# Pairwise products of 40 projected features: two input buffers and growing stores, against four input buffers and twelve equal stores a tile

## The chip, the cores and the metric

The kernel runs on one core of a Trainium2 chip, the others idle. The metric is the device time in microseconds (us) of one execution. Before the change the median of three runs is 506.32 us (506.20 to 506.38). The profiled execution took 506.18 us, of which the profile's span covers 504.4 us.

## The reference

The input `r_x` is 512 x 40 x 128 in float32 and `W` is 128 x 128. Each of the 40 features of a sample is projected with `W`, and the output holds the elementwise product of each of the 780 pairs of projected features:

```
proj = jnp.einsum('bnd,ed->bne', x, W)          # 512 x 40 x 128
out = proj[:, PAIR_I, :] * proj[:, PAIR_J, :]   # 512 x 780 x 128, pairs i < j
```

The input has 10.5 MB, the output 204.5 MB.

## The kernel before

The 512 samples are cut into four tiles of 128, one sample to a partition. The five engines run programs written out by hand, and semaphores alone set the order between them.

**Loads.** SyncE (SP in the profile) issues all transfers but that of W. Tile 0 is loaded in three pieces (`FIRST_LOADS`), then tile 1 (L111). `feats` has two halves; tile t lives in half t % 2. Tiles 2 and 3 are loaded later (L122): SP issues each once all stores of tile t - 2 are issued, since the products of that tile were then computed and its half is free. They stand in the same queue as the stores.

**Projection.** TensorE turns two features at a time (L140), ScalarE carries them to SBUF (L189), TensorE multiplies them by the turned W (L149), and ScalarE writes the result over the features in `feats` (L195). This goes in groups of two features from feature 39 down. From tile 1 on, TensorE waits for the tile's load first (L173).

**Products.** VectorE (DVE) goes through the pairs from the last to the first. Pairs with one i are one instruction (L212), cut where a chunk ends. A chunk is what one store moves. It is written into one of three slots (`products0` to `products2`), and VectorE waits before each chunk until the store that last used its slot has landed (L222 in tile 0, L227 in the loop over tiles 1 to 3). For tile 0 there are 15 chunks that grow from 30 to 69 pairs (`FIRST_SIZES`), for each later tile nine chunks of 87 or 86 pairs (`SIZES`).

**Stores.** SP waits until a chunk is ready (L117) and issues its store (L118), 42 stores in all. One pair of one tile is 64 KB (128 partitions x 512 bytes). SP waits for the last three stores at the end (L126).

Of the kernel before, what the change touches and what calls it, by code (L numbers as in the profile page):

```python
# [5 lines left out]
P = 128  # L6
FEATURES = 40
DIM = 128
PAIRS = FEATURES * (FEATURES - 1) // 2
FIRST_PAIR = [i * (FEATURES - 1) - i * (i - 1) // 2 for i in range(FEATURES)]  # L10

GROUP = 2
# [4 lines left out]
FIRST_LOADS = [(36, 40), (28, 36), (0, 28)]  # L17

SLOTS = 3
FIRST_SIZES = [30, 34, 38, 41, 44, 47, 50, 53, 56, 59, 62, 64, 66, 67, 69]
SIZES = [87] * 6 + [86] * 3
SLOT_PAIRS = max(FIRST_SIZES + SIZES)
FIRST_ROUNDS = len(FIRST_SIZES) // SLOTS
ROUNDS = len(SIZES) // SLOTS

assert sum(FIRST_SIZES) == PAIRS and sum(SIZES) == PAIRS
assert FIRST_ROUNDS * SLOTS == len(FIRST_SIZES) and ROUNDS * SLOTS == len(SIZES)
assert GROUPS * GROUP == FEATURES and GROUPS % 2 == 0 and GROUP <= BANK_FEATURES  # L30


# [5 lines left out]
    return (FEATURES - 1 - i) // GROUP  # L38


def chunk_ranges(sizes):

    ranges, high = [], PAIRS
    for size in sizes:
        ranges.append((high - size, high))
        high -= size
    return ranges


def chunk_rows(low, high):  # L50

    rows = []
    for i in reversed(range(FEATURES - 1)):
        a, b = max(low, FIRST_PAIR[i]), min(high, FIRST_PAIR[i + 1])
        if a < b:
            rows.append((i, i + 1 + a - FIRST_PAIR[i], b - a, a - low))
    return rows


def pairwise_products(nc, x, w, out):  # L60
    fp32 = mybir.dt.float32
    ALU = mybir.AluOpType
    tiles = x.shape[0] // P
    assert x.shape[0] == tiles * P and tiles % 2 == 0 and tiles >= 4

    first_chunks = chunk_ranges(FIRST_SIZES)
    chunks = chunk_ranges(SIZES)

    with ExitStack() as ctx:  # L69
        def sbuf(name, shape):  # L70
            return ctx.enter_context(nc.sbuf_tensor(name, shape, fp32))
# [4 lines left out]
        def sem(name):  # L76
            return ctx.enter_context(nc.semaphore(name))


        feats = sbuf("feats", [P, 2, FEATURES, DIM])  # L80
        products = [sbuf(f"products{s}", [P, SLOT_PAIRS, DIM]) for s in range(SLOTS)]
        x_turned = [sbuf(f"x_turned{k}", [DIM, GROUP, P]) for k in range(2)]
        w_in = sbuf("w_in", [DIM, DIM])
        w_turned = sbuf("w_turned", [DIM, DIM])
        identity = sbuf("identity", [P, P])
# [4 lines left out]

        w_loaded = sem("w_loaded")
        first_loaded = [sem(f"first_loaded{k}") for k in range(len(FIRST_LOADS))]
        tile_loaded = [sem(f"tile_loaded{half}") for half in range(2)]
        identity_zeroed = sem("identity_zeroed")
        identity_made = sem("identity_made")
        w_in_ps = sem("w_in_ps")
# [10 lines left out]
        @block.sync  # L107
        def _(sp):
            for k, (a, b) in enumerate(FIRST_LOADS):
                sp.dma_start(feats[:, 0, a:b, :], x[0:P, a:b, :]).then_inc(first_loaded[k], 16)  # L110
            sp.dma_start(feats[:, 1, :, :], x[P:2 * P, :, :]).then_inc(tile_loaded[1], 16)  # L111

            done = 0
            for tile in range(tiles):
                for k, (a, b) in enumerate(first_chunks if tile == 0 else chunks):
                    done += 1
                    sp.wait_ge(chunk_ready, done)  # L117
                    sp.dma_start(out[tile * P:(tile + 1) * P, a:b, :],  # L118
                                 products[k % SLOTS][:, 0:b - a, :]).then_inc(stored[k % SLOTS], 16)
                if tile + 2 < tiles:  # L120

                    sp.dma_start(feats[:, tile % 2, :, :],  # L122
                                 x[(tile + 2) * P:(tile + 3) * P, :, :]).then_inc(tile_loaded[tile % 2], 16)

            for slot in range(SLOTS):
                sp.wait_ge(stored[slot], 16 * (FIRST_ROUNDS + (tiles - 1) * ROUNDS))  # L126

        @block.gpsimd
        def _(pool):
# [4 lines left out]

        @block.tensor
        def _(pe):
            def turn(half, group):
                a, b = group_range(group)
                for n in range(a, b):
                    last = pe.transpose(turned_ps[group % 2][:, n - a, :], feats[:, half, n, :], identity[:, :])  # L140
                last.then_inc(group_turned, 1)

            def project(before, group):
                pe.wait_ge(x_turned_ready, before + (group + 1))
                if group >= 2:

                    pe.wait_ge(proj_ready, before + (group - 1))
                for k in range(GROUP):
                    last = pe.matmul(proj_ps[group % 2][:, k, :], x_turned[group % 2][:, k, :], w_turned[:, :],  # L149
                                     start=True, stop=True)  # L150
                last.then_inc(group_projected, 1)

            def last_banks_left(before):
                pe.wait_ge(proj_ready, before + GROUPS)

            pe.wait_ge(identity_made, 1)
            pe.wait_ge(w_loaded, 16)
            pe.transpose(w_ps[:, :], w_in[:, :], identity[:, :]).then_inc(w_in_ps, 1)  # L158

            starts = {group_of(b - 1): k for k, (a, b) in enumerate(FIRST_LOADS)}  # L160
            pe.wait_ge(first_loaded[0], 16)
            turn(0, 0)
            pe.wait_ge(w_ready, 1)
            for group in range(1, GROUPS):
                if group in starts:
                    pe.wait_ge(first_loaded[starts[group]], 16)
                turn(0, group)
                project(0, group - 1)
            project(0, GROUPS - 1)
            last_banks_left(0)  # L170

            for tile in range(1, tiles):
                pe.wait_ge(tile_loaded[tile % 2], 16 * ((tile + 1) // 2) if tile % 2 else 16 * (tile // 2))  # L173
                turn(tile % 2, 0)
                for group in range(1, GROUPS):
                    turn(tile % 2, group)
                    project(tile * GROUPS, group - 1)
                project(tile * GROUPS, GROUPS - 1)
                last_banks_left(tile * GROUPS)

        @block.scalar
        def _(act):
            act.dma_start(w_in[:, :], w).then_inc(w_loaded, 16)
            act.wait_ge(w_in_ps, 1)
            act.copy(w_turned[:, :], w_ps[:, :]).then_inc(w_ready, 1)  # L185

            def carry_turned(tile, group):
                act.wait_ge(group_turned, tile * GROUPS + group + 1)
                act.copy(x_turned[group % 2][:, :, :], turned_ps[group % 2][:, 0:GROUP, :]).then_inc(x_turned_ready, 1)  # L189

            def carry_projected(tile, group):

                a, b = group_range(group)
                act.wait_ge(group_projected, tile * GROUPS + group + 1)
                act.copy(feats[:, tile % 2, a:b, :], proj_ps[group % 2][:, 0:GROUP, :]).then_inc(proj_ready, 1)  # L195

            for tile in range(tiles):
                carry_turned(tile, 0)
                for group in range(1, GROUPS):
                    carry_turned(tile, group)  # L200
                    carry_projected(tile, group - 1)
                carry_projected(tile, GROUPS - 1)

        @block.vector
        def _(dve):
            def multiply_chunk(tile, k, low, high, seen):

                for i, j, count, place in chunk_rows(low, high):
                    if group_of(i) >= seen:
                        seen = group_of(i) + 1  # L210
                        dve.wait_ge(proj_ready, tile * GROUPS + seen)  # L211
                    last = dve.tensor_tensor(  # L212
                        products[k % SLOTS][:, place:place + count, :],
                        feats[:, tile % 2, i:i + 1, :].broadcast_to([P, count, DIM]),
                        feats[:, tile % 2, j:j + count, :], ALU.mult)
                last.then_inc(chunk_ready, 1)
                return seen

            seen = 0
            for k, (low, high) in enumerate(first_chunks):  # L220
                if k >= SLOTS:
                    dve.wait_ge(stored[k % SLOTS], 16 * (k // SLOTS))  # L222
                seen = multiply_chunk(0, k, low, high, seen)
            with dve.Fori(1, tiles) as tile:  # L224
                seen = 0
                for k, (low, high) in enumerate(chunks):
                    dve.wait_ge(stored[k % SLOTS],  # L227
                                16 * ROUNDS * tile + 16 * (FIRST_ROUNDS - ROUNDS + k // SLOTS))
                    seen = multiply_chunk(tile, k, low, high, seen)


# [19 lines left out]
```

## Time and profile before

| what | value |
|---|---|
| median of 3 runs | 506.32 us |
| profiled execution, its own time | 506.18 us |
| span of its profile | 504.4 us |
| VectorE busy | 431.6 us (86%) |
| TensorE busy / ScalarE busy | 66.4 us / 54.7 us |
| moved by the DMA engines | 215.11 MB, 426 GB/s over the span |
| read from HBM / written to HBM | 10.55 MB / 204.47 MB |
| VectorE waiting for a store to land | 36.6 us |
| SP waiting for a chunk of products | 457.7 us |

A queue's share in the profile is the time that its packets took, divided by the time that 16 DMA engines have in the span: close to 100% means that the engines hardly ever stood still. SP's wait for products is no loss by itself, since SP waits while earlier stores are still being moved. The GB/s of a short stretch is rough by a few GB/s, because a store's packets are large (43.5 KB in a store of 87 pairs) and 16 of them are under way at a time.

### The profile page before, as it was taken

How to read it: one execution, taken by the hardware profiler on the slowest of the kernel's cores; microseconds unless marked ns; L12 is line 12 of the kernel's file. 1: busy time of each engine (PE TensorE's matmuls, PEld its weight loads, DVE VectorE, ACT ScalarE, POOL GpSimd, SP SyncE). 2: the span in 40 equal slices, each digit the busy share in tenths (PEclk: the TensorE clock that was granted, in tenths of full speed). 3: DMA queues.
4: the chain of work that ended last, by engine and by line, in shares of the span. 5: the costliest groups of instructions: out<-in, count | busy, mean ns of one | idle time of the engine just before them, and what ended most of it. 6: DMA issues, size and time to landing. Idle time of an engine off the chain costs nothing.

```text
span 504.4 us, 1671 instructions
## 1 busy us (share of the span) xinstructions
PE 66.4 (13%) x481; PEld 60.9 (12%) x481; DVE 431.6 (86%) x191; ACT 54.7 (11%) x162; POOL 0.7 (0%) x6
## 2 busy tenths in 40 slices
PE   6990000000067000000007500000000000000000
PEld 6880000000057000000007500000000000000000
DVE  3999999999996989888996788988899998988800
ACT  5880000000036000000005500000000000000000
POOL 0000000000000000000000000000000000000000
PEclk9995555555559555555557955555555555555555
DMA  8999999999999999999999999999999999999997
GB/s 350 428 435 425 429 434 432 444 428 437 384 404 439 442 424 435 442 435 419 440 421 455 413 439 445 420 435 441 433 423 440 442 424 435 442 427 429 440 443 307
DMA packets 7062, 215.11 MB, mean 426 GB/s; under 512 B 784, under 2 KB 912, under 8 KB 1168
## 3 DMA queue, kind: packets, MB, share of 16 engines
q1 hardware_dynamic: 6912, 214.96, 99.3%
q10 hardware_dynamic: 144, 0.07, 0.0%
q8 instruction: 4, 0.07, 0.0%
q14 instruction: 2, 0.02, 0.0%
HBM read 10.55 MB, written 204.47 MB: 426 GB/s over the span
## 4 chain that ended last, share of the span: by engine, by line
DMA 46%; DVE 41%; issue 5%; DVEq 2%; PE 1%; ACT 0%
DMA out_dram<-products 45%; DVE products L212 41%; DVEq L69 1%; DMA w_in<-in_L_rec_W_dram 1%; PE proj_ps L149 1%; DVEq L212 0%; PE turned_ps L140 0%; DVEq L211 0%; DVEq L224 0%; PE w_ps L158 0%; ACT feats L195 0%; DVEq L227 0%
## 5 line engine op out<-in xcount | busy, mean ns | idle before, releaser
L212 DVE TENSOR_TENSOR products<-feats 128x384 f32 (+49 forms) x191 | 431.6, 2331 | 45.1 <-DMA out_dram<-products 36.6
L140 PE MATMUL turned_ps<-identity,feats 128*128 128x128 f32 x160 | 33.3, 297 | 213.8 <-DMA feats<-in_r_x_dram 213.3
L149 PE MATMUL proj_ps<-w_turned,x_turned 128*128 128x128 f32 x320 | 56.9, 304 | 0.3 <-ACT x_turned L189 0.2
L189 ACT COPY x_turned<-turned_ps 128x256 f32<-128x256 f32 x80 | 30.1, 378 | 215.3 <-PE turned_ps L140 214.8
L140 PEld LDWEIGHTS turned_ps<-identity,feats 128*128 128x128 f32 x160 | 22.1, 156 | 214.6 <-issue 213.6
L149 PEld LDWEIGHTS proj_ps<-w_turned,x_turned 128*128 128x128 f32 x320 | 45.5, 205 | 4.8 <-ACT x_turned L189 2.0
L195 ACT COPY feats<-proj_ps 128x256 f32<-128x256 f32 x80 | 29.8, 372 | 11.8 <-PE proj_ps L149 6.6
L185 ACT ACT_TABLE_LOAD x1 | 1.3, 1283 | 1.2 <-PEq L240 1.2
L158 PE MATMUL w_ps<-identity,w_in 128*128 128x128 f32 x1 | 0.4, 444 | 4.1 <-DMA w_in<-in_L_rec_W_dram 4.1
L158 PEld LDWEIGHTS w_ps<-identity,w_in 128*128 128x128 f32 x1 | 0.2, 183 | 4.1 <-issue 4.1
L185 ACT COPY w_turned<-w_ps 128x128 f32<-128x128 f32 x1 | 0.3, 265 | 2.2 <-PE w_ps L158 2.2
L132 POOL TENSOR_SCALAR_AFFINE_SELECT identity<-identity 128x128 f32<-128x128 f32 x1 | 0.3, 293 | 0.2 <-POOL identity L130 0.2
L130 POOL MEMSET identity<- 128x128 f32 x1 | 0.2, 205 | 0.3 <-POOLq L240 0.3
L240 POOL MEMSET const-bfloat16-1.0<- 128x1 bf16 x1 | 0.1, 101 | 0.0
L240 POOL MEMSET const-uint8-127<- 128x1 uint8 x1 | 0.1, 101 | 0.0
L240 POOL MEMSET const-float32-0.0<- 128x1 f32 x1 | 0.1, 98 | 0.2 <-issue 0.2
L240 POOL MEMSET const-float32-1.0<- 128x1 f32 x1 | 0.1, 98 | 0.0
## 6 DMA issues: line engine op xcount, KB each, us to landing
out_dram<-products SPq DMA_DIRECT2D x18, 5568.0 KB, 27.5
out_dram<-products SPq DMA_DIRECT2D x9, 5504.0 KB, 27.3
feats<-in_r_x_dram SPq DMA_DIRECT2D x3, 2560.0 KB, 26.8
out_dram<-products SPq DMA_DIRECT2D x1, 4416.0 KB, 18.9
out_dram<-products SPq DMA_DIRECT2D x1, 4288.0 KB, 17.7
out_dram<-products SPq DMA_DIRECT2D x1, 4224.0 KB, 16.7
out_dram<-products SPq DMA_DIRECT2D x1, 4096.0 KB, 15.8
out_dram<-products SPq DMA_DIRECT2D x1, 3968.0 KB, 14.8
```

The source lines that it names most:

```text
L69: with ExitStack() as ctx:
L130: pool.memset(identity[:, :], 0.0).then_inc(identity_zeroed, 1)
L132: pool.affine_select(out=identity[:, :], in_=identity[:, :], compare_op=ALU.not_equal, fill=1.0, base=0, pattern=[[-1, P]], channel_multip ...
L140: last = pe.transpose(turned_ps[group % 2][:, n - a, :], feats[:, half, n, :], identity[:, :])
L149: last = pe.matmul(proj_ps[group % 2][:, k, :], x_turned[group % 2][:, k, :], w_turned[:, :], start=True, stop=True)
L158: pe.transpose(w_ps[:, :], w_in[:, :], identity[:, :]).then_inc(w_in_ps, 1)
L185: act.copy(w_turned[:, :], w_ps[:, :]).then_inc(w_ready, 1)
L189: act.copy(x_turned[group % 2][:, :, :], turned_ps[group % 2][:, 0:GROUP, :]).then_inc(x_turned_ready, 1)
L195: act.copy(feats[:, tile % 2, a:b, :], proj_ps[group % 2][:, 0:GROUP, :]).then_inc(proj_ready, 1)
L212: last = dve.tensor_tensor(products[k % SLOTS][:, place:place + count, :], feats[:, tile % 2, i:i + 1, :].broadcast_to([P, count, DIM]), f ...
L240: nc = _bacc.Bacc("TRN2", target_bir_lowering=False, num_devices=1)
```

## The change

`feats` gets one buffer per tile, four in all. SP issues the loads of tiles 1, 2 and 3 directly behind those of tile 0, all on one semaphore, `tiles_loaded`, and no load between the stores. TensorE waits once, before tile 1, until all three have landed. A tile's projections are written over its own buffer, as before. All tiles have the same twelve chunks of 65 pairs, so there are 48 stores; the three slots shrink from 87 to 65 pairs. Pairs, products and their order are the same.

```diff
-FIRST_SIZES = [30, 34, 38, 41, 44, 47, 50, 53, 56, 59, 62, 64, 66, 67, 69]
-SIZES = [87] * 6 + [86] * 3
+CHUNK = 65
+CHUNKS = PAIRS // CHUNK
+ROUNDS = CHUNKS // SLOTS
...
-        feats = sbuf("feats", [P, 2, FEATURES, DIM])
-        products = [sbuf(f"products{s}", [P, SLOT_PAIRS, DIM]) for s in range(SLOTS)]
+        feats = sbuf("feats", [P, tiles, FEATURES, DIM])
+        products = [sbuf(f"products{s}", [P, CHUNK, DIM]) for s in range(SLOTS)]
...
-            sp.dma_start(feats[:, 1, :, :], x[P:2 * P, :, :]).then_inc(tile_loaded[1], 16)
-            done = 0
+            for tile in range(1, tiles):
+                sp.dma_start(feats[:, tile, :, :], x[tile * P:(tile + 1) * P, :, :]).then_inc(tiles_loaded, 16)
...
-                if tile + 2 < tiles:
-                    sp.dma_start(feats[:, tile % 2, :, :],
-                                 x[(tile + 2) * P:(tile + 3) * P, :, :]).then_inc(tile_loaded[tile % 2], 16)
...
+            pe.wait_ge(tiles_loaded, 16 * (tiles - 1))
             for tile in range(1, tiles):
-                pe.wait_ge(tile_loaded[tile % 2], 16 * ((tile + 1) // 2) if tile % 2 else 16 * (tile // 2))
...
-                for k, (low, high) in enumerate(chunks):
-                    dve.wait_ge(stored[k % SLOTS],
-                                16 * ROUNDS * tile + 16 * (FIRST_ROUNDS - ROUNDS + k // SLOTS))
-                    seen = multiply_chunk(tile, k, low, high, seen)
+                for k in range(CHUNKS):
+                    dve.wait_ge(stored[k % SLOTS], 16 * ROUNDS * tile + 16 * (k // SLOTS))
+                    seen = multiply_chunk(tile, k, seen)
```

The queue of SP before, from the load of tile 1 into the stores of tile 1; 128x3840 is a store of 30 pairs (128 elements each):

```order
L111 DMA feats<-in_r_x_dram 128x5120
L118 DMA out_dram<-products 128x3840 [waits chunk_ready]
L118 DMA out_dram<-products 128x4352 [waits chunk_ready]
...
L118 DMA out_dram<-products 128x8576 [waits chunk_ready]
L118 DMA out_dram<-products 128x8832 [waits chunk_ready]
L122 DMA feats<-in_r_x_dram 128x5120
L118 DMA out_dram<-products 128x11136 [waits chunk_ready] x6
```

The whole queue of SP in the changed kernel:

```order
L96 UNCONDITIONAL_BRANCH [waits barrier_Pool_Activation_PE_DVE_SP_release]
L99 DMA feats<-in_r_x_dram 128x512
L99 DMA feats<-in_r_x_dram 128x1024
L99 DMA feats<-in_r_x_dram 128x3584
L101 DMA feats<-in_r_x_dram 128x5120 x3
L107 DMA out_dram<-products 128x8320 [waits chunk_ready] x48
L57 UNCONDITIONAL_BRANCH [waits stored2,stored1,stored0]
```

The two later loads moved ahead of the first store, and the stores became 48 equal ones.

VectorE's first chunk before ends with the row of 128x256 (1 + 2 + ... + 7 + 2 = 30 pairs):

```order
L212 TENSOR_TENSOR products<-feats 128x640
L212 TENSOR_TENSOR products<-feats 128x768 [waits proj_ready]
L212 TENSOR_TENSOR products<-feats 128x896
L212 TENSOR_TENSOR products<-feats 128x256 [waits proj_ready]
L212 TENSOR_TENSOR products<-feats 128x768
L212 TENSOR_TENSOR products<-feats 128x1152
```

In the changed kernel it ends with the first of the two rows of 128x1280 (1 + 2 + ... + 10 + 10 = 65 pairs):

```order
L197 TENSOR_TENSOR products<-feats 128x640
L197 TENSOR_TENSOR products<-feats 128x768 [waits proj_ready]
L197 TENSOR_TENSOR products<-feats 128x896
L197 TENSOR_TENSOR products<-feats 128x1024 [waits proj_ready]
L197 TENSOR_TENSOR products<-feats 128x1152
L197 TENSOR_TENSOR products<-feats 128x1280 [waits proj_ready]
L197 TENSOR_TENSOR products<-feats 128x1280
```

The products are computed in the same order, and the point at which the first store may go moved from the 30th pair to the 65th.

## Rows read from the trace of the kernel before

**Rows 1.** The page's DMA rows: the span in 40 slices, then queue q1.
```profile
DMA  8999999999999999999999999999999999999997
GB/s 350 428 435 425 429 434 432 444 428 437 384 404 439 442 424 435 442 435 419 440 421 455 413 439 445 420 435 441 433 423 440 442 424 435 442 427 429 440 443 307
...
q1 hardware_dynamic: 6912, 214.96, 99.3%
```

**Rows 2.** SP's timeline, single windows: start us, us, the DMA issued.
```profile
13.25 0.35 SPq L118 DMA_DIRECT2D out_dram<-products  x1
...
18.05 0.34 SPq L118 DMA_DIRECT2D out_dram<-products  x1
...
116.72 1.24 SPq L122 DMA_DIRECT2D feats<-in_r_x_dram  x1
...
476.76 0.33 SPq L118 DMA_DIRECT2D out_dram<-products  x1
```

**Rows 3.** Waits of VectorE and SP in total: us, times, longest us.
```profile
DVE products L212 <- DMA out_dram<-products: 36.6, 22, 7.5
...
SPq L126 <- DMA out_dram<-products: 26.8, 1, 26.8
```

**Rows 4.** Stretches: length, each engine's busy us, PEclk, DMA share, GB/s.
```profile
2.00:27.00 25.00, 22.17 (x161) 20.14 (x161) 18.60 (x19) 17.86 (x54) 0.00 (x0) 1.00 1.02 425
...
27.00:130.00 103.00, 10.18 (x83) 9.22 (x81) 103.00 (x50) 9.21 (x29) 0.00 (x0) 0.56 1.01 432
...
115.00:145.00 30.00, 1.32 (x5) 0.95 (x6) 30.00 (x23) 0.61 (x2) 0.00 (x0) 0.50 1.02 411
...
130.00:145.00 15.00, 1.32 (x5) 0.95 (x6) 15.00 (x8) 0.61 (x2) 0.00 (x0) 0.50 1.01 384
...
245.00:280.00 35.00, 12.09 (x85) 11.37 (x86) 27.64 (x15) 9.08 (x28) 0.00 (x0) 0.62 0.99 425
...
270.00:480.00 210.00, 14.64 (x114) 13.75 (x112) 182.62 (x69) 12.58 (x38) 0.00 (x0) 0.54 1.00 434
```

**Rows 5.** The page's DMA issues: count, KB each, median us from issue to landing.
```profile
out_dram<-products SPq DMA_DIRECT2D x18, 5568.0 KB, 27.5
...
feats<-in_r_x_dram SPq DMA_DIRECT2D x3, 2560.0 KB, 26.8
...
out_dram<-products SPq DMA_DIRECT2D x1, 4224.0 KB, 16.7
```

**Rows 6.** VectorE's timeline: start us, us, instructions, idle before and its releaser.
```profile
183.18 11.89 DVE L212 TENSOR_TENSOR products<-feats 128x3840 f32 x3 [1.40 <-DMA out_dram<-products]
196.12 11.83 DVE L212 TENSOR_TENSOR products<-feats 128x768 f32 x4 [1.04 <-DMA out_dram<-products]
209.25 11.76 DVE L212 TENSOR_TENSOR products<-feats 128x2816 f32 x3 [1.30 <-DMA out_dram<-products]
222.39 11.76 DVE L212 TENSOR_TENSOR products<-feats 128x1152 f32 x3 [1.38 <-DMA out_dram<-products]
235.79 24.82 DVE L212 TENSOR_TENSOR products<-feats 128x128 f32 x20 [1.63 <-DMA out_dram<-products]
261.38 12.03 DVE L212 TENSOR_TENSOR products<-feats 128x2048 f32 x5 [0.77 <-DMA out_dram<-products]
```

**Rows 7.** VectorE's instructions by shape: busy us in total, mean ns of one.
```profile
L212 DVE TENSOR_TENSOR products<-feats 128x4992 f32 x3 | 16.1, 5351 | 0.0
...
L212 DVE TENSOR_TENSOR products<-feats 128x1920 f32 x6 | 12.9, 2155 | 12.5 <-DMA out_dram<-products 12.5
```

**Rows 8.** Timeline of TensorE and ScalarE: tile 1's first turn, tile 3's last copy.
```profile
21.86 0.66 PE L140 MATMUL turned_ps<-identity,feats 128*128 128x128 f32 x4 [0.46 <-ACT feats L195]
...
284.70 0.37 ACT L195 COPY feats<-proj_ps 128x256 f32<-128x256 f32 x1 [0.36 <-PE proj_ps L149]
```

More of the change, by code:

```diff
@@ L21 @@
 SLOTS = 3
-FIRST_SIZES = [30, 34, 38, 41, 44, 47, 50, 53, 56, 59, 62, 64, 66, 67, 69]
-SIZES = [87] * 6 + [86] * 3
[L24 to L29, printed above, removed]
+CHUNK = 65
+CHUNKS = PAIRS // CHUNK
+ROUNDS = CHUNKS // SLOTS
+assert CHUNKS * CHUNK == PAIRS and ROUNDS * SLOTS == CHUNKS
 assert GROUPS * GROUP == FEATURES and GROUPS % 2 == 0 and GROUP <= BANK_FEATURES
@@ L38, in group_of, with chunk_range @@
     return (FEATURES - 1 - i) // GROUP
[L41 to L47, printed above, removed]
+def chunk_range(k):
+    return PAIRS - (k + 1) * CHUNK, PAIRS - k * CHUNK
 def chunk_rows(low, high):
@@ L63, in pairwise_products @@
     tiles = x.shape[0] // P
-    assert x.shape[0] == tiles * P and tiles % 2 == 0 and tiles >= 4
-    first_chunks = chunk_ranges(FIRST_SIZES)
-    chunks = chunk_ranges(SIZES)
+    assert x.shape[0] == tiles * P and 2 <= tiles <= 4
     with ExitStack() as ctx:
@@ L92, in pairwise_products @@
         first_loaded = [sem(f"first_loaded{k}") for k in range(len(FIRST_LOADS))]
-        tile_loaded = [sem(f"tile_loaded{half}") for half in range(2)]
+        tiles_loaded = sem("tiles_loaded")
         identity_zeroed = sem("identity_zeroed")
@@ L110, in _ @@
                 sp.dma_start(feats[:, 0, a:b, :], x[0:P, a:b, :]).then_inc(first_loaded[k], 16)
-            sp.dma_start(feats[:, 1, :, :], x[P:2 * P, :, :]).then_inc(tile_loaded[1], 16)
-            done = 0
+            for tile in range(1, tiles):
+                sp.dma_start(feats[:, tile, :, :], x[tile * P:(tile + 1) * P, :, :]).then_inc(tiles_loaded, 16)
             for tile in range(tiles):
[L115 to L119, printed above, removed]
-                if tile + 2 < tiles:
-                    sp.dma_start(feats[:, tile % 2, :, :],
-                                 x[(tile + 2) * P:(tile + 3) * P, :, :]).then_inc(tile_loaded[tile % 2], 16)
+                for k in range(CHUNKS):
+                    low, high = chunk_range(k)
+                    sp.wait_ge(chunk_ready, tile * CHUNKS + k + 1)
+                    sp.dma_start(out[tile * P:(tile + 1) * P, low:high, :],
+                                 products[k % SLOTS][:, :, :]).then_inc(stored[k % SLOTS], 16)
             for slot in range(SLOTS):
-                sp.wait_ge(stored[slot], 16 * (FIRST_ROUNDS + (tiles - 1) * ROUNDS))
+                sp.wait_ge(stored[slot], 16 * tiles * ROUNDS)
         @block.gpsimd
@@ L136, in _, with turn @@
         def _(pe):
-            def turn(half, group):
+            def turn(tile, group):
                 a, b = group_range(group)
                 for n in range(a, b):
-                    last = pe.transpose(turned_ps[group % 2][:, n - a, :], feats[:, half, n, :], identity[:, :])
+                    last = pe.transpose(turned_ps[group % 2][:, n - a, :], feats[:, tile, n, :], identity[:, :])
                 last.then_inc(group_turned, 1)
@@ L170, in _ @@
             last_banks_left(0)
+            pe.wait_ge(tiles_loaded, 16 * (tiles - 1))
             for tile in range(1, tiles):
-                pe.wait_ge(tile_loaded[tile % 2], 16 * ((tile + 1) // 2) if tile % 2 else 16 * (tile // 2))
-                turn(tile % 2, 0)
+                turn(tile, 0)
                 for group in range(1, GROUPS):
-                    turn(tile % 2, group)
+                    turn(tile, group)
                     project(tile * GROUPS, group - 1)
@@ L194, in carry_projected @@
                 act.wait_ge(group_projected, tile * GROUPS + group + 1)
-                act.copy(feats[:, tile % 2, a:b, :], proj_ps[group % 2][:, 0:GROUP, :]).then_inc(proj_ready, 1)
+                act.copy(feats[:, tile, a:b, :], proj_ps[group % 2][:, 0:GROUP, :]).then_inc(proj_ready, 1)
             for tile in range(tiles):
@@ L205, in _, with multiply_chunk @@
         def _(dve):
-            def multiply_chunk(tile, k, low, high, seen):
-                for i, j, count, place in chunk_rows(low, high):
+            def multiply_chunk(tile, k, seen):
+                for i, j, count, place in chunk_rows(*chunk_range(k)):
                     if group_of(i) >= seen:
@@ L213, in multiply_chunk @@
                         products[k % SLOTS][:, place:place + count, :],
-                        feats[:, tile % 2, i:i + 1, :].broadcast_to([P, count, DIM]),
-                        feats[:, tile % 2, j:j + count, :], ALU.mult)
+                        feats[:, tile, i:i + 1, :].broadcast_to([P, count, DIM]),
+                        feats[:, tile, j:j + count, :], ALU.mult)
                 last.then_inc(chunk_ready, 1)
@@ L219, in _ @@
             seen = 0
-            for k, (low, high) in enumerate(first_chunks):
+            for k in range(CHUNKS):
                 if k >= SLOTS:
                     dve.wait_ge(stored[k % SLOTS], 16 * (k // SLOTS))
-                seen = multiply_chunk(0, k, low, high, seen)
+                seen = multiply_chunk(0, k, seen)
             with dve.Fori(1, tiles) as tile:
                 seen = 0
-                for k, (low, high) in enumerate(chunks):
-                    dve.wait_ge(stored[k % SLOTS],
-                                16 * ROUNDS * tile + 16 * (FIRST_ROUNDS - ROUNDS + k // SLOTS))
-                    seen = multiply_chunk(tile, k, low, high, seen)
+                for k in range(CHUNKS):
+                    dve.wait_ge(stored[k % SLOTS], 16 * ROUNDS * tile + 16 * (k // SLOTS))
+                    seen = multiply_chunk(tile, k, seen)
 _INS = ["r_x", "L0_rec_W"]
```

## The prediction

> **What bounds the kernel now.** I read the page's DMA rows first. Queue q1, which carries all loads of x and all stores, holds the 16 DMA engines for 99.3% of the span, and every slice but the first and the last reads 9 [rows 1]. Then I asked who waits. VectorE waits 36.6 us in all for stores to land [rows 3], so it is not the bound; SP issues the last store at 476.76 us and then waits 26.8 us for it [rows 2, 3]. So the bound is the stream of bytes through the DMA engines, from the first load to the last store. The reader should see that both kernels move the same 10.5 MB in and 204.5 MB out. The change can act on the time only in three ways: the stream runs dry, its rate changes, or its start and end change.
>
> The third view is the rate by stretch [rows 4]. The stream runs at 434 GB/s from 270 to 480 us, where stores of 86 and 87 pairs go, and at 432 from 27 to 130 us, where tile 0's smaller stores go. It dips twice, at the two places where a load passes between stores. From 130 to 145 us it is 384, the low slices 384 and 404 of the page [rows 1]. As the stretch ahead of it reads high (packets are counted whole), I use both together: 411 from 115 to 145 us. SP issued tile 2's load at 116.72 us [rows 2], and loads land 26.8 us after their issue in the middle one of three [rows 5], so about 143 us. The dip ends when the load does. Tile 3's load leaves a much smaller mark: 425 from 245 to 280 us.
>
> **The change part by part.** All sums are made against the span of 504.4 us. The profiled execution took 506.18 us, so 1.8 us lie around its span, and it is 0.14 us under the median of 506.32.
>
> *The loads of tiles 2 and 3 leave the stores.* Their 5.2 MB move to the start, where only loads are under way; their own time moves along and is no gain. The gain is the dips. Tile 2's: 30 us at 411 instead of 434 GB/s is 30 x 23 / 434 = 1.6 us, against 432 it is 1.5 us. Tile 3's: 35 x 9 / 434 = 0.7 us at most; by the row's roughness (one round of 16 packets of 43.5 KB is 0.7 MB, so 20 GB/s over 35 us) it may as well be nothing, and 0.1 is what I take for it. That the dip belongs to mixing load and stores, and not to the reading of tile 2 as such, is not shown by the trace: tile 3's load, in the same position, hardly dips. If it belongs to the tile, it comes again at the start. The bounds are 0 and 2.3 us of gain. I take 1.6.
>
> *Six more stores.* There were 42, there are 48, all of 65 pairs (4.26 MB). Does a smaller store move more slowly per byte? The lower bound is nothing: the 434 GB/s of the large ones holds. The upper bound is the 432 of tile 0's stores, which average 52 pairs (and of which the one nearest in size, 66 pairs, shows nothing special: 16.7 us from issue to landing, with part of its predecessor ahead of it [rows 5]). Tiles 1 to 3 write 153.4 MB: 153.4 / 432 - 153.4 / 434 = 355.0 - 353.4 = 1.6 us. A part of the 432 may stem from something else in that stretch, so I take the middle, 0.8 us of loss.
>
> *A rule against this change.* Between stores of 87 pairs VectorE's waits end every 13.1 us (starts 183.18, 196.12, 209.25, 222.39) [rows 6], and 5.70 MB in 13.1 us is 434 GB/s, so nothing is paid between one store and the next that is queued behind it. The Trainium skill, DMA: Bandwidth & Descriptors, section "Anatomy of one DMA", gives each DMA about 2.0 us fixed beside bytes / 436 GB/s; if these added up in the queue, six more stores would cost 12 us as an estimate from that page. The trace says that this fixed part lies beside the next store: it is seen in landings only, 27.5 us for two times 13.1, thus 1.2 us.
>
> *Does the stream run dry at the start?* Before, the first store is issued at 13.25 us, when the 5.2 MB of two tiles are through [rows 2]. Now 10.5 MB are ahead: at the 425 GB/s of the first stretch [rows 4] they last 24.7 us from 2 us on, to about 27 us. The first chunk ends at pair 65; before, the 64th pair's store went out at 18.05 us [rows 2], and the order of products is the same, so the first store is issued at about 18.2 us, 9 us early. The second needs one more chunk. An instruction costs 1.04 ns per element and 0.16 us (5351 ns for 4992 elements, 2155 for 1920) [rows 7], so a chunk of 8320 elements is 8.7 us and 3 to 11 instructions: 9.1 to 10.4 us. It is ready at 27.5, while the first store lasts until 27 + 9.8 = 37 us.
>
> *Does it run dry later?* A store of 65 pairs takes 4.26 / 434 = 9.8 us. A slot is free when its store has landed, 1.2 us after its last byte; two stores, of 19.6 us, are then queued, so VectorE has 19.6 - 1.2 = 18.4 us for the next chunk. It needs 9.1 to 10.4. Before it had 26.3 - 1.2 = 25.1 and needed 11.8 to 12.4 (24.82 us for the two chunks at a tile's start, with 20 instructions) [rows 6]. The margin falls from 13 to 8 us and covers what lies around a chunk: the idle rows ahead of a chunk are 0.8 to 1.6 us [rows 6]. Cost: nothing. VectorE's waits shrink by nothing that matters either.
>
> *TensorE's single wait.* It started tile 1 at 21.86 us [rows 8]; now it waits until all loads have landed, at 28 to 29 us. Behind that wait stand all turns and products of tiles 1 to 3, and ScalarE's copies. VectorE needs the first of tile 1 only after 780 pairs, thus after its twelfth chunk, about 115 us or later. A tile takes TensorE 16 us (tile 1: about 22 to 38), so all are done near 80 us, instead of 284.70 [rows 8]. Cost: nothing, hidden behind tile 0's products.
>
> *The end.* SP issues the last store about 21 us before the end instead of 26.8; the queue is full until then and the landing of 1.2 us is the same. No gain.
>
> *Sum.* 504.4 - 1.6 + 0.8 = 503.6 us of span, 505.4 as the profiled execution counts, and 505.5 beside the median of 506.32. That is 0.16% less, and a measurement of this kernel can't tell less than 0.2% (1.0 us) from no change. The forecast is: no change that can be measured, with the gain of the unmixed loads half eaten by smaller stores.
>
> **The rivals.** *Faster, 504.7 us.* Small stores go at 434 as well, and both dips go: 506.32 - 1.6 = 504.7, and 504.0 if tile 3's whole 0.7 counts. For it: a fixed price between stores is nowhere seen, and queued loads alone show no dip. Against it: the 432 of tile 0.
>
> *Slower, 507.9 us.* The dip is tile 2's read and comes again, and stores of 65 pairs go at tile 0's rate throughout: 506.32 + 1.6. It decides from 507.3 on, thus when the dip stays and small stores cost at least 1.0 us. For it: tile 3's load in the same place shows nearly no dip, so mixing alone does not explain tile 2's. Against it: the three runs agree within 0.2 us, and the dip lasts just as long as a load.
>
> *Slower by a dry stream, 509 to 515 us.* If VectorE needs more than the 18.4 us for a chunk, each us beyond is lost on every such chunk. At each start of the loop over tiles (three times) a loss of 1 to 3 us would give 3 to 9 us. It needs 8 us above the 10.4 of the longest chunk; no row shows idle time of this size except 7.5 us once, waiting for a store [rows 3].
>
> *The dip stays and small stores are free*: 506.3, no change, like the forecast in the time.
>
> **How the numbers follow.** Dip gone, 0.65; stores of 65 pairs dearer by over 0.8 us, 0.45. This gives: faster (dip gone, stores free or nearly) 0.36; dip gone and stores dear, 505.5 to 506.3, 0.28; dip stays, stores free, 0.18; both against it, 0.14; dry stream 0.04. The second and third lie within 0.2%, with 0.02 of the first: forecast of no change 0.45, faster than 505.3 us 0.38, slower than 507.3 us 0.17. The range leaves out the dry stream and the ends of the others: 504.4 to 507.9 us.
>
> **What would show it.** In the changed profile q1's share stays at 99%, the slice digits are all 9, the landing of a store is 19.6 + 1.2 = 20.8 us, and the first three slices hold all loads. No slice in the middle falls under 410 GB/s if mixing was the cause; a low slice within the first 27 us would show that tile 2's read itself is slow. The rate in the middle is 434 if small stores are free and 432 if not. The forecast is wrong by a dry stream if SP's waits end and DMA digits under 9 stand in the middle, above all at a tile's start.

## The result and the profile after

The changed kernel takes 505.76 us (median of 22 runs, 505.34 to 506.02), the kernel before 506.46 in as many runs beside it (505.94 to 506.99). The ratio is 0.9987, its 95% interval 0.9981 to 0.9993: faster by 0.7 us, or 0.13%. That is clear of zero, though it is less than the 0.2% that the prediction took for the smallest change that can be told. The profiled execution has a span of 503.8 us (504.4 before).

The page's DMA rows of the changed kernel, in 40 slices of 12.6 us, and queue q1:

```profile
DMA  8999999999999999999999999999999999999997
GB/s 356 424 403 441 427 424 429 447 428 425 434 444 428 428 433 444 428 428 431 447 428 428 431 447 428 428 431 441 433 428 428 436 439 431 428 428 439 433 433 312
...
q1 hardware_dynamic: 7776, 214.96, 99.3%
```

As in [rows 1], the stream of bytes is the bound, and all slices but the outer two read 9. The low slices 384 and 404 are gone from the middle. A low slice, 403, now stands at 25 to 38 us.

The rate by stretch of the changed kernel; the columns are those of [rows 4]:

```profile
15.00:21.00 6.00, 5.96 (x48) 5.35 (x46) 6.00 (x5) 5.05 (x16) 0.00 (x0) 1.00 1.02 437
21.00:27.00 6.00, 0.00 (x0) 0.00 (x0) 6.00 (x5) 0.37 (x1) 0.00 (x0) 0.79 1.05 385
...
24.00:30.00 6.00, 0.00 (x0) 0.00 (x0) 6.00 (x5) 0.00 (x0) 0.00 (x0) 0.54 0.99 355
...
115.00:145.00 30.00, 0.00 (x0) 0.00 (x0) 27.84 (x20) 0.00 (x0) 0.00 (x0) 0.50 1.02 438
...
245.00:280.00 35.00, 0.00 (x0) 0.00 (x0) 32.29 (x25) 0.00 (x0) 0.00 (x0) 0.50 1.00 433
270.00:480.00 210.00, 0.00 (x0) 0.00 (x0) 192.60 (x80) 0.00 (x0) 0.00 (x0) 0.50 1.00 433
```

Against [rows 4]: 115 to 145 us went from 411 to 438, 245 to 280 from 425 to 433. The long stretch of stores went from 434 to 433. The new dip is at 21 to 30 us, in the last of the three large loads; the one before it, at 15 to 21 us, runs at 437. The size of a dip can be read from such a row only roughly: a second profile of the changed kernel (g3 below) has 409 where this one has 385. From here on the text therefore also uses the packet records of the traces, the start, size and duration of each packet. A packet of these loads has 20480 bytes and takes 761 ns in the median. "Slow" is one that takes over 60 ns more than is usual for its size, and the sum of such excess, divided by the 16 engines, is what a stall cost.

Landings, waits and VectorE's rhythm after the change, from the page's DMA issues, the waits in total and VectorE's timeline:

```profile
out_dram<-products SPq DMA_DIRECT2D x48, 4160.0 KB, 20.5
```
```profile
DVE products L197 <- DMA out_dram<-products: 41.1, 42, 5.4
...
PE turned_ps L125 <- DMA feats<-in_r_x_dram: 10.3, 1, 10.3
...
SPq L111 <- DMA out_dram<-products: 20.2, 1, 20.2
```
```profile
119.70 8.89 DVE L197 TENSOR_TENSOR products<-feats 128x3328 f32<-128x3328 f32 x2 [0.89 <-DMA out_dram<-products]
129.87 18.65 DVE L197 TENSOR_TENSOR products<-feats 128x128 f32 x17 [1.27 <-DMA out_dram<-products]
149.18 9.10 DVE L197 TENSOR_TENSOR products<-feats 128x768 f32 x5 [0.66 <-DMA out_dram<-products]
159.02 9.03 DVE L197 TENSOR_TENSOR products<-feats 128x1920 f32 x4 [0.74 <-DMA out_dram<-products]
```

VectorE starts a chunk every 9.84 us, as long as a store lasts, and waits 0.7 to 1.3 us before it [rows 6 before: 0.8 to 1.6]. Where 17 instructions stand together, at a tile's start, two chunks take 18.65 us. TensorE's one wait of 10.3 us is seen and nobody waits for it: VectorE's two waits for projections, 8.0 us in all, are both in tile 0, before 9 us.

### The profile page after: what moved, and what is told of

It reads as the page before. It is cut to its first block, busy times and chain, and to the rows that moved or that the text cites. A ratio compares the mean times of both kernels' runs of the same rounds, so it can differ in the third digit from the quotient of the medians.

```text
span 503.8 us, 1684 instructions
## 1 busy us (share of the span) xinstructions
PE 63.4 (13%) x481; PEld 57.6 (11%) x481; DVE 433.6 (86%) x196; ACT 54.2 (11%) x162; POOL 0.7 (0%) x6
## 3 DMA queue, kind: packets, MB, share of 16 engines
q1 hardware_dynamic: 7776, 214.96, 99.3%
## 4 chain that ended last, share of the span: by engine, by line
DMA 62%; DVE 25%; issue 5%; DVEq 2%; PE 1%; ACT 0%
DMA out_dram<-products 62%; DVE products L197 25%; DVEq L57 2%; DMA w_in<-in_L_rec_W_dram 1%; PE proj_ps L134 0%; PE turned_ps L125 0%; DVEq L197 0%; DVEq L196 0%; DVEq L209 0%; PE w_ps L143 0%; ACT feats L180 0%; DVEq L212 0%
## 5 line engine op out<-in xcount | busy, mean ns | idle before, releaser
L197 DVE TENSOR_TENSOR products<-feats 128x1280 f32 (+36 forms) x196 | 433.6, 2275 | 49.2 <-DMA out_dram<-products 41.1
L134 PE MATMUL proj_ps<-w_turned,x_turned 128*128 128x128 f32 x320 | 54.7, 295 | 0.6 <-ACT x_turned L174 0.5
L134 PEld LDWEIGHTS proj_ps<-w_turned,x_turned 128*128 128x128 f32 x320 | 43.3, 197 | 5.3 <-ACT x_turned L174 2.1
L125 PE MATMUL turned_ps<-identity,feats 128*128 128x128 f32 x160 | 31.7, 285 | 11.3 <-DMA feats<-in_r_x_dram 10.3
L125 PEld LDWEIGHTS turned_ps<-identity,feats 128*128 128x128 f32 x160 | 20.9, 148 | 12.3 <-issue 10.5
## 6 DMA issues: line engine op xcount, KB each, us to landing
out_dram<-products SPq DMA_DIRECT2D x48, 4160.0 KB, 20.5
```

Of the source, the lines that this page charges most:

```text
L197: last = dve.tensor_tensor(products[k % SLOTS][:, place:place + count, :], feats[:, tile, i:i + 1, :].broadcast_to([P, count, DIM]), feats ...
```

## The experiments

Each run is compared with the kernel before on the same chip, and is an edit of the kernel before, of the changed kernel or of another run. The times are medians; "before" had 506.27 us beside e1 to e4, 506.36 beside f1 to f5 and 506.44 beside g1 to g3.

### The two halves of the change, apart (e1, e2)

e1 is the kernel before with one line changed:

```diff
-SIZES = [87] * 6 + [86] * 3
+SIZES = [65] * 12
```

> The kernel before with only the stores of tiles 1 to 3 changed, from nine of 87 or 86 pairs to twelve of 65; loads and tile 0 as before, 51 stores in all. Theory A (a packet costs a fixed 8 ns beside its bytes, so a store costs 0.07 us, from the packets of 33280 bytes at 1232 ns and of 44544 bytes at 1646 ns): nine more stores give +0.6 us, 507.1. Theory B (small stores move at tile 0's 432 instead of 434 GB/s): +1.6 us, 508.1. Theory C (store size costs nothing): 506.5. The stall near 132 to 142 us, while tile 2's load is under way, stays in A and B alike.

Measured: 507.05 us against 506.27, ratio 1.0016 (1.0007 to 1.0025). Nine stores more cost 0.8 us, 0.09 us each. That is theory A (507.1) and not B (508.1): the interval ends at 0.25%, and B asked for 0.32%. It leaves out C (506.5) too.

e2 adds to e1 the four buffers, the loads in front and TensorE's single wait, and leaves tile 0's growing stores. The part of its edit that moves the loads:

```diff
-            sp.dma_start(feats[:, 1, :, :], x[P:2 * P, :, :]).then_inc(tile_loaded[1], 16)
+            for tile in range(1, tiles):
+                sp.dma_start(feats[:, tile, :, :], x[tile * P:(tile + 1) * P, :, :]).then_inc(tiles_loaded, 16)
...
-                if tile + 2 < tiles:
-                    sp.dma_start(feats[:, tile % 2, :, :],
-                                 x[(tile + 2) * P:(tile + 3) * P, :, :]).then_inc(tile_loaded[tile % 2], 16)
```

> The first experiment's kernel with all four tiles loaded first into four buffers; tile 0 keeps its 15 growing stores, the others have twelve of 65. Theory A (the gain is the stall of a load that passes between stores): 1 to 1.5 us faster than the first experiment, about 505.8, a little above the changed kernel (3 stores more, +0.2). Rival (the gain is the equal stores of tile 0, the loads' place is worth nothing): equal to the first experiment. In the trace a smaller stall, about 1 us, is expected in the last load as in the changed kernel, 23 to 29 us.

Measured: 505.87 us, ratio 0.9993 (0.9984 to 1.0002). Against e1 this is 1.2 us less, and the rival (no difference from e1) is out: the place of the loads is the gain. (TensorE's wait came with it; f2 below shows that it is worth nothing that can be told.) Two rows of each trace, e1 first, show where it lies: the stretch that holds tile 2's load in e1, and in e2 the last of the loads in front.

```profile
20.00:30.00 10.00, 9.22 (x74) 8.15 (x73) 10.00 (x7) 7.87 (x25) 0.00 (x0) 1.00 1.02 431
130.00:145.00 15.00, 0.92 (x4) 0.71 (x4) 13.55 (x8) 0.23 (x1) 0.00 (x0) 0.50 0.98 368
```
```profile
20.00:30.00 10.00, 0.74 (x5) 0.52 (x4) 2.80 (x2) 0.79 (x3) 0.00 (x0) 0.72 0.99 386
130.00:145.00 15.00, 0.00 (x0) 0.00 (x0) 15.00 (x14) 0.00 (x0) 0.00 (x0) 0.50 1.01 436
```

The 15 us at 368 GB/s are worth 2.3 us against 434, the 10 us at 386 are worth 1.1 us. By the packets it is 1.9 and 0.9 us. So a stall of some 2 us was exchanged for one of some 1 us. VectorE was busy for 2.80 of the 10 us in e2 and for all of them in the changed kernel, and the stall by the packets is 0.9 and 1.0 us: VectorE's work does not cause it.

The packets also show why the stall in the middle was the larger one: it has two parts, one ahead of each change of kind. In the kernel before, the last packets of the store ahead of tile 2's load are slow already (13 of the 15 that began at 132 to 133 us, up to 2465 ns where 1307 are usual; 0.6 us), although the load's first packet begins only at 134.28 us. The load's own packets then lose 1.1 us, most of it from 138 us on, and the next store's first packet begins at 141.32. In e1 the two parts are 0.55 and 1.4 us. A load in front of all stores has only the second part.

### The price of a store (e3, e4)

Only `CHUNK` is changed in the changed kernel, to 52 (60 stores) and to 26 (120 stores).

```diff
-CHUNK = 65
+CHUNK = 52
```

> The changed kernel with 15 stores of 52 pairs a tile, 60 in all. At 0.07 us a store: +0.8 us over the changed kernel, 506.6. If small stores lose 0.4% of their rate instead and 65 pairs already do so: no further loss, 505.8.

Measured: 506.47 us, ratio 1.0002 (0.9993 to 1.0011).

> The changed kernel with 30 stores of 26 pairs a tile, 120 in all. At 0.07 us a store: 72 more give +5 us, 510.8. The time that VectorE has for a chunk is 2 x 3.93 - 1.2 = 6.7 us by the trace's landing of 1.2 us behind the last byte; a chunk needs 3.7 to 4.5 us, so the stream does not run dry, except possibly at a tile's start, where it would show as DMA digits under 9.

Measured: 512.09 us, ratio 1.0112 (1.0097 to 1.0128). With 505.8 for 48 stores, 12 more cost 0.7 us (0.06 each) and 72 more 6.3 us (0.09 each). e3 came as expected (506.6); e4 was expected at 510.8 and is 1.3 us above that. The theory of a lower rate that 65 pairs already have (505.8, no further loss) is out by e4; e3 alone, whose interval touches that of the changed kernel, would not have decided. The rate of 270 to 480 us falls with the size of the stores, e3 first, then e4:

```profile
270.00:480.00 210.00, 0.00 (x0) 0.00 (x0) 193.05 (x87) 0.00 (x0) 0.00 (x0) 0.50 1.00 431
```
```profile
270.00:480.00 210.00, 0.00 (x0) 0.00 (x0) 194.26 (x114) 0.00 (x0) 0.00 (x0) 0.50 1.01 425
```

The DMA share stays at 1.00 and 1.01, so the engines never stood still; they paid more for the same bytes. The packet records say the same: the median packet takes 500 ns for 13312 bytes, 987 for 26624, 1232 for 33280 and 1646 for 44544. From the last two, 11264 bytes are 414 ns, so 33280 bytes alone are 1223 ns, and 9 ns are left for each of the 8 packets that a store puts on an engine. That is 0.07 us a store. For the small packets of e4 it is too little: 13312 bytes alone would be 489 ns, which leaves 11 ns a packet in the median and 14 in the mean, thus 0.09 to 0.11 us a store. This is what e4's expectation had too low.

Even with 26 pairs the stream did not run dry. VectorE's timeline in e4 shows chunks of 3.7 us every 3.9 us; it waits for landings before nearly all of them:

```profile
38.44 3.76 DVE L197 TENSOR_TENSOR products<-feats 128x128 f32<-128x128 f32 x3 [0.27 <-DMA out_dram<-products]
42.43 3.76 DVE L197 TENSOR_TENSOR products<-feats 128x768 f32<-128x768 f32 x3 [0.22 <-DMA out_dram<-products]
46.35 3.69 DVE L197 TENSOR_TENSOR products<-feats 128x1920 f32<-128x1920 f32 x2 [0.16 <-DMA out_dram<-products]
```

### Whose stall is it? (f2, f4, f5, f1)

f2 gives each load its own semaphore, and TensorE waits per tile.

```diff
-            pe.wait_ge(tiles_loaded, 16 * (tiles - 1))
             for tile in range(1, tiles):
+                pe.wait_ge(tile_loaded[tile], 16)
```

> The changed kernel with one semaphore per tile's load, so that TensorE goes on to tile 1 at about 21.9 us instead of waiting for all loads until about 32 us. Theory A (TensorE's wait is hidden behind tile 0's products): same time as the changed kernel, 505.7 us, and the stall in tile 3's load at 23 to 29 us stays. Rival D (the stall comes with TensorE standing still or with its program being fetched at about 22 us): the stall goes or moves, and the time falls by up to 1 us.

Measured: 505.57 us, ratio 0.9980 (0.9971 to 0.9989), which can't be told from the changed kernel's 0.9987 (0.9981 to 0.9993). The dip stays, with TensorE at work in it for 5.57 of 6 us, and by the packets it costs 0.85 us:

```profile
22.00:28.00 6.00, 5.57 (x45) 5.06 (x46) 6.00 (x4) 4.62 (x15) 0.00 (x0) 1.00 1.04 382
```

Rival D is out.

f4 and f5 are f2 with tile 3's load put behind the stores of tile 0 or of tile 1:

```diff
-            for tile in range(1, tiles):
+            for tile in range(1, tiles - 1):
                 sp.dma_start(feats[:, tile, :, :], x[tile * P:(tile + 1) * P, :, :]).then_inc(tile_loaded[tile], 16)
...
+                if tile == 0:     # f5: tile == 1
+                    sp.dma_start(feats[:, 3, :, :], x[3 * P:4 * P, :, :]).then_inc(tile_loaded[3], 16)
```

> The changed kernel with tile 3's load issued behind the stores of tile 0, as tile 2's load was before; loads of tiles 1 and 2 stay in front; TensorE waits per tile. Position theory (the place in the store stream causes the stall): tile 3's load stalls by 1.7 us near 130 to 145 us and nothing stalls in front: 506.3 to 506.5. Address theory (tile 2's read is slow beside stores, tile 3's is not): no stall, about 504.8. Theory of the time since the start (the stall comes at 23 us in any kernel that reads then): none of both, since no load runs at 23 us; about 504.8 as well.

> As the last one, with tile 3's load issued behind the stores of tile 1, where it was before. Before, the load in this place cost 0.1 us by its packets. Position theory: no stall of more than 0.2 us anywhere, about 504.8 us, the fastest of all. If the stall belongs to the third or the last load of a row of loads, whatever it is, it shows in tile 2's load, 15 to 21 us, and the time stays at 505.7.

Measured: f4 506.12 us, ratio 0.9993 (0.9984 to 1.0003); f5 506.68 us, 1.0008 (0.9999 to 1.0018). f4 is near the position theory (506.3 to 506.5) and far from the two others (504.8). f5 fails everything that was expected of it (504.8 or 505.7): it is the slowest of the kernels with 48 stores and no added load or wait, and tile 3's load stalls in the very place where it lost 0.1 us before. The stretches around the late load, first f4, then f5:

```profile
135.00:150.00 15.00, 0.71 (x4) 0.72 (x4) 14.36 (x9) 0.01 (x1) 0.00 (x0) 0.50 0.98 386
...
245.00:275.00 30.00, 0.00 (x0) 0.00 (x0) 28.09 (x22) 0.00 (x0) 0.00 (x0) 0.50 1.00 430
```
```profile
125.00:152.00 27.00, 0.00 (x0) 0.00 (x0) 25.60 (x18) 0.00 (x0) 0.00 (x0) 0.50 1.00 432
...
250.00:265.00 15.00, 0.00 (x0) 0.00 (x0) 14.36 (x10) 0.00 (x0) 0.00 (x0) 0.50 0.99 379
```

The dip goes where the load goes, with tile 3 as with tile 2, at 140 as at 258 us. So neither the tile's address nor the time since the start nor the place in the row of stores decides. By the packets the late load and the store ahead of it lose 1.2 us in f4 and 1.6 us in f5. Both kernels also lose 0.3 us in front, in the last packets of tile 2's load (14 and 9 slow packets), where the first store was issued about 3 to 4 us before that load's last packet began. The sums, 1.5 and 1.9 us, stand beside 0.85 us in f2, and the times are 0.55 and 1.1 us above f2's: the packets account for the order of the three kernels and for most of the differences.

f1 is the changed kernel with one small load more behind the three large ones:

```diff
+        spare = sbuf("spare", [P, 12, DIM])
...
+            sp.dma_start(spare[:, :, :], x[0:P, 0:12, :]).then_inc(spare_loaded, 16)
```

> The changed kernel with one load more at the end of the front, 12 features of tile 0 into a spare buffer (0.79 MB, 16 x 8 packets of 6144 bytes). All theories: the time rises by the bytes, 0.79 MB / 434 = 1.8 us, 507.5, since the stream is the bound and the first store waits behind the loads. If the stall marks the switch from the last load to the first store, it moves behind 27 us into the small load; if it comes at 23 us whatever is behind, it stays in tile 3's load.

Measured: 507.65 us, ratio 1.0025 (1.0016 to 1.0034), 1.9 us above the changed kernel where its bytes are worth 1.8. The stream is the bound here too. The dip moved back:

```profile
21.00:27.00 6.00, 0.74 (x5) 0.52 (x4) 6.00 (x4) 0.79 (x3) 0.00 (x0) 0.98 0.99 421
...
26.00:32.00 6.00, 1.20 (x5) 0.83 (x5) 6.00 (x4) 0.48 (x2) 0.00 (x0) 0.57 1.02 372
```

In the changed kernel these two stretches read 385 and 396. The packets are plainer: in tile 3's load 4 are slow and it loses 0.13 us (30 to 34 and 0.8 to 1.0 us in the changed kernel), and in the small load 51 of 128 are slow and it loses 0.8 us. The stall is in whatever load is last ahead of a queued store. It need not be large: tile 1's load in the kernel before, last in front as well, has no slow packet; its first store was issued at 13.25 us, 1.4 us before the load's last packet began.

### The stall without the store behind it, and mixed (g2, g1, g3)

In g2 SP issues the first store only when all loads have landed:

```diff
+            sp.wait_ge(tiles_loaded, 16 * (tiles - 1))
             for tile in range(tiles):
```

> The changed kernel, where SP issues the first store only when all loads have landed. The stream then stands still for the landing and one issue, 1.5 to 2.5 us. If the stall of 1 us in the last load comes from the store queued behind it, the stall goes: 506.2 to 507.2. If it does not, 507.3 to 508.3, and the last load still has packets far above 761 ns.

Measured: 507.74 us, ratio 1.0026 (1.0015 to 1.0036). The time is in the range of the second case, yet the trace shows the first: the last load is quick. Tile 3's load, from its issue at about 3.3 us to its landing, in g2, and then in g3, which is the changed kernel again (505.74 us, ratio 0.9985, 0.9976 to 0.9994), and in the changed kernel's first profile:

```profile
feats<-in_r_x_dram SPq DMA_DIRECT2D x1, 2560.0 KB, 26.1
```
```profile
feats<-in_r_x_dram SPq DMA_DIRECT2D x1, 2560.0 KB, 26.8
```
```profile
feats<-in_r_x_dram SPq DMA_DIRECT2D x1, 2560.0 KB, 28.1
```

By the packet records, 1 packet of the last load in g2 took over 60 ns more than the 761 ns of its size, 30 in g3, 34 in the changed kernel; summed and divided by the 16 engines that is 0.03, 0.8 and 1.0 us. So the stall at the end of a load needs a store queued right behind it. (A load queued behind is not enough: none of the 256 packets of tiles 1 and 2 in the changed kernel is slow.) What went wrong in the expectation is the price of the gap, 2.0 us net with the stall of 1 us gone: the engines stand still for about 3 us in the mean, shown by the stretch of 24 to 30 us, 208 GB/s at a DMA share of 0.49, half of six us. Only 1.3 us of this lie between the end of the load's last packet (28.80 us) and the first packets of the store (30.08); the rest is that most engines are through with the load 1 to 2 us earlier and have nothing to go on with.

```profile
24.00:30.00 6.00, 0.65 (x3) 0.68 (x4) 6.00 (x5) 0.00 (x0) 0.00 (x0) 0.59 0.49 208
```

> The changed kernel once more, beside the two others on the same chip: 505.7, and again a stall of about 1 us in the last load (packets of 20480 bytes above 761 ns between 23 and 29 us), if the stall belongs to the program and not to chance.

g3 gives both numbers again, so time and stall belong to the program and not to chance.

g1 asks whether reads beside writes are slow as such. It is e2 with tiles 2 and 3 loaded from ScalarE's queue while stores run, and TensorE waits per tile:

```diff
                 carry_projected(tile, GROUPS - 1)
+                if tile == 0:
+                    for later in range(2, tiles):
+                        act.dma_start(feats[:, later, :, :],
+                                      x[later * P:(later + 1) * P, :, :]).then_inc(tile_loaded[later], 16)
```

> The kernel of e2 (tile 0 with its 15 growing stores, the others with twelve of 65), but tiles 2 and 3 are loaded from ScalarE's queue, issued at about 21 us when tile 0 is projected, so that their packets go between the stores' packets for some 24 us; only tiles 0 and 1 are loaded in front. TensorE waits per tile. Switch theory (time is lost where all engines go over from loads to stores or back): the front switch costs nothing as before (0.0), and the mixed stretch costs little: 505.0 to 505.4. Mixing theory (reads beside writes are slow as such, 0.1 to 0.2 us per us of load): the mixed stretch of 24 us loses 3 us or more, 508.5 or above.

Measured: 506.19 us, ratio 0.9996 (0.9987 to 1.0005), 0.8 us above the range of the switch theory and over 2 us below that of the mixing theory. The loads last from 24 to 50 us, and their first six us are slow while the rest is not:

```profile
24.00:30.00 6.00, 5.89 (x49) 5.54 (x49) 4.80 (x3) 5.00 (x17) 0.00 (x0) 1.00 1.02 356
30.00:48.00 18.00, 17.29 (x140) 15.82 (x140) 12.02 (x6) 14.98 (x47) 0.00 (x0) 1.00 1.01 431
```

18 us of packets of both kinds side by side run at 431 GB/s. Mixing in itself costs nothing that can be seen here; the beginning of it costs, 6 x (434 - 356) / 434 = 1.1 us, and the switch theory had not counted this. That g1 and e2 can't be told apart in time (0.9996 and 0.9993) agrees.

## Why the prediction was right, and where it was not

The forecast was 505.5 us and no change that can be measured; 505.76 and a ratio of 0.9987 came out. The two terms of its sum had the right sign and were both too large, the gain by 0.4 us and the loss by 0.3 us. That the errors cancel, and -0.8 us stands beside the measured -0.7, is luck; a wide range (504.4 to 507.9) helped as well. By its steps:

- **The bound.** Right. Share 99.3%, digits of 9, and f1's added bytes cost 1.9 us for 1.8 worked out.
- **The loads leave the stores, -1.6 us.** The kind of gain was right, its size too large: e1 to e2 gives -1.2 us. The term missed that the loads in front meet the stores once as well: a new stall of about 1 us against some 2 us taken away. So of its two cases, the dip gone (0.65) or the dip back, neither came: half of it came back. The assumption under the term was that the dip is "mixing load and stores". g1 shows that mixing is not it, g2 that a store queued behind the load is, for the part at the load's end. The prediction also took the whole dip for the load's own time; it begins at 132 us, 2 us before the load's first packet, in the store ahead.
- **The alternative that it belongs to reading tile 2.** The text would have taken a low slice within the first 27 us as proof of it. Such a slice came, 403 at 25 to 38 us, and would have misled: the slow packets are tile 3's and not tile 2's, and f4 and f5 show the dip following tile 3's load through the kernel.
- **Six more stores, 0 to 1.6 us, 0.8 taken.** Right in kind; e1 and e4 give 0.09 us a store, thus 0.5 us. The price goes with the number of stores (each has 128 packets, so stores and packets can't be told apart), and the 432 GB/s of tile 0's stores, from which the term came, is not a rate that they all have: 60 to 100 us of the kernel before, tile 0's stores too, run at 434. Put together: -1.2 + 0.5 = -0.7 us, the measured difference; each of the two numbers is known to half a microsecond at best, so the agreement to a tenth says little.
- **The rule on the fixed part of a DMA.** The Trainium skill, DMA: Bandwidth & Descriptors, section "Anatomy of one DMA", gives about 2.0 us per DMA, fitted to transfers that GpSimd issues; the prediction left that condition out, and SyncE issues the transfers here. For queued stores the runs disagree with adding it up: 72 more stores cost 6.3 us and not 144. In the landing, 1.2 us before the change and about 0.8 after it (20.5 - 2 x 9.84), less than that figure is seen.
- **No dry stream.** Right at the start (the first store was issued at 17.61 us, worked out as 18.2, and its first packet began at 27.76, worked out as 27) and later. e4 shows that even 26 pairs, where the same working leaves 2 to 3 us, keep it full.
- **TensorE's wait.** Right: f2 takes it away and gains nothing that can be told. It ended at 31.3 us and not at 28 to 29, since the stall and the landing of the last load were not in the sum; the margin to 115 us swallows this.
- **The end.** SP's last wait was worked out as 21 us, and is 20.2.

The rival "faster, 504.7" failed since half of the dip came back and the stores were not free; "slower, 507.9" failed on the price of the stores, and since the dip that came back is the smaller one. The chances in the prediction do not follow from its own table either, which adds up to 0.48 for no change, 0.34 for faster and 0.18 for slower, where 0.45, 0.38 and 0.17 are given.

What stays open is why the stall has different sizes: by the packet records 1.75 us around tile 2's load and 0.1 around tile 3's in the kernel before, but 1.6 us for f5's load in that same place; in front, none at tile 1's load before, 0.3 us at tile 2's in f4 and f5, and 0.8 to 1.0 us at tile 3's in the changed kernel. In front the stall is larger where the store has been queued longer behind the load (issued 1.4, 3 to 4 and over 10 us before the load's last packet), but in the middle this does not hold: tile 3's load before had a store queued behind it for 10 us ahead of its first packet. Nor do the runs say by what mechanism a queued store slows the load ahead of it. The part in the store ahead of a load was not tested by a run of its own. A version with the loads in front and stores of 87 pairs, which would join both gains, was not tried: four buffers of 20 KB and three slots of 43.5 KB a partition are 210 KB, and the largest layout that was run here has 187 KB a partition.

## What to carry to other kernels

When one stream of bytes fills the DMA engines, price a change in two coins: the number of transfers (here 0.06 to 0.09 us each, with 128 packets apiece) and the number of times that the stream goes over from one kind to the other (here 0 to 1.4 us each, two of them for a load between stores). Moving loads to the front does not remove the last of these changes, it moves it there, so look in the first stretch for a part of what was saved in the middle. And when a dip has a place and a cause is guessed, move the suspect: one load put elsewhere told more than any row of the first trace.

## What the hardware showed that was not expected

- A load slows down before the store behind it has moved: in the changed kernel 26 of the 30 load packets that began at 25 to 27 us are slow, and the store's first packet begins at 27.76 us; in g3 it is 26 of 34, and 27.72. In g2, with no store queued, none of the 38 of that stretch is. The rates alone would not have shown it: 21 to 27 us read 416 GB/s in g2 and 409 in g3, the two rows below, and 385 in the changed kernel's first profile.

```profile
21.00:27.00 6.00, 0.57 (x4) 0.38 (x4) 6.00 (x5) 0.63 (x2) 0.00 (x0) 0.84 0.98 416
```
```profile
21.00:27.00 6.00, 0.94 (x7) 0.56 (x5) 6.00 (x4) 0.99 (x3) 0.00 (x0) 0.73 1.08 409
```

- The same goes for a store with a load queued behind it: its last packets are slow at 132 to 133 us of the kernel before, and the load's first packet begins at 134.28 us.
- Loads and stores whose packets run side by side from two queues go at 431 GB/s (g1, 30 to 48 us), about as fast as stores alone (433 and 434), after 6 us at 356.
- A gap in which no transfer is queued, for one landing and one issue, costs 3 us of the engines' time in the mean (g2), of which 1.3 us lie behind the last packet; the kernel is 2.0 us slower by it, since the stall of 1 us is gone.
